# A graph network of two layers: in the attention layer VectorE's two 1280-wide passes change places, and TensorE turns the scores before it sums over edges

## The reference

```
h = relu(layernorm(x));  x = x + attention(h)      # 4 heads of 32
h = relu(layernorm(x));  x = x + messages(h)

attention:
  q, k, v = h@Wq+bq, h@Wk+bk, h@Wv+bv
  alpha[e,head] = sum_c q[dst]*k[src] / sqrt(32)
  alpha = softmax of alpha over the edges with one dst
  out[n] = sum over edges into n of v[src]*alpha  +  h@Wskip + bskip
```

## Time and profile before

| what | value |
|---|---|
| median of 3 timed runs | 1677.4 us (1675.71 to 1679.96) |
| the profiled execution, from first to last instruction | 2119.4 us |
| table stage, in the profile | 0 to about 344 us |
| attention layer | about 344 to 1204 us |
| start of the message layer | about 1204 to 1303 us |
| message layer | about 1303 to 2107 us |
| busy over the span: PE, DVE, ACT, POOL | 75%, 66%, 49%, 47% |

### The profile page before, as it was taken

The page is one execution under the profiler, slowest core; times in us unless marked ns, Lnnn a source line. Parts: engine busy times, 40 slices in busy tenths (PEclk is TensorE's granted clock), DMA queues, the critical chain, the costliest instruction groups (busy, mean ns, idle before and its releaser), DMA issues.

```text
span 2119.4 us, 34578 instructions
## 1 busy us (share of the span) xinstructions
PE 1596.5 (75%) x10545; PEld 1337.9 (63%) x10546; DVE 1390.2 (66%) x3977; ACT 1036.2 (49%) x2500; POOL 990.1 (47%) x1021
## 2 busy tenths in 40 slices
PE   5879964877788777778877515877788887788887
PEld 4667753767777777777776414666566665666665
DVE  8998951777778777777778703555555555555565
ACT  6668963444444444444444023544444444444453
POOL 0100005655566566656664074555555555555530
PEclk9989996999999999999999757999888888777789
DMA  8778974445454555545454233545444445444442
GB/s 239 242 237 275 316 231 123 124 137 150 127 148 137 144 148 140 148 132 147 135 146 127 62 96 72 129 118 122 120 116 116 119 119 123 123 119 121 117 109 62
DMA packets 162399, 302.86 MB, mean 143 GB/s; under 512 B 104084, under 2 KB 107674, under 8 KB 157245
## 3 DMA queue, kind: packets, MB, share of 16 engines
q1 hardware_dynamic: 121349, 201.19, 32.6%
q0 software_dynamic: 40896, 99.90, 18.7%
HBM read 196.84 MB, written 104.12 MB: 142 GB/s over the span
## 4 chain that ended last, share of the span: by engine, by line
PE 47%; DVE 19%; issue 17%; another core or an unknown queue 10%; DMA 2%; ACT 2%; SPq 1%; DVEq 0%; ACTq 0%
PE ps_b L1769 6%; PE ps_b L1877 5%; PE ps_b L1888 5%; PE ps_b L1889 5%; PE ps_b L1890 5%; PE ps_b L1865 4%; PE ps_b L1899 4%; PE ps_b L1670 3%; DVE sb_member L1055 2%; PE ps_b L1802 2%; PE ps_b L1876 2%; PE ps_b L1757 2%; DVE sb_st L833 1%; DVE sb_kv L854 1%
## 5 line engine op out<-in xcount | busy, mean ns | idle before, releaser
L749 POOL DMA_INDIRECT sb_kv<-kv_rows,sb_src_all x500 | 504.1, 1008 | 542.2 <-DMA kv_rows<-sb_kv 207.1
L777 POOL DMA_INDIRECT sb_kv<-x_rows,sb_src_all x500 | 473.3, 947 | 420.1 <-ACT sb_vw L1586 228.8
L1583 ACT ACTIVATE sb_hn<-sb_xn 100x128 f32<-100x128 f32 x500 | 243.7, 487 | 498.4 <-PE ps_b L1877 241.8
L1274 DVE COPY sb_hT<-ps_b 128x400 f32<-128x400 f32 x250 | 142.2, 569 | 202.3 <-remote 155.0
L1586 ACT ACTIVATE sb_vw<-sb_kv 128x128 f32<-128x128 f32 x500 | 241.1, 482 | 0.0
L1511 ACT ACTIVATE sb_hn<-sb_xn,sb_nstat 100x128 f32<-100x128 f32 x500 | 231.7, 495 | 13.7 <-DMA sb_xn<-in_x 13.7
L1899 PE MATMUL ps_b<-sb_ident,sb_q 128*100 128x128 f32 x500 | 99.8, 324 | 156.6 <-issue 111.7
L1670 PE MATMUL ps_b<-sb_w,sb_memberT 128*125 128x256 f32 x800 | 203.1, 392 | 17.3 <-DVE sb_kv L854 13.9
L1802 PE MATMUL ps_b<-sb_vw,sb_member 128*100 128x128 f32 x1000 | 139.4, 290 | 68.2 <-DVE sb_vw L1115 68.2
L1533 ACT COPY sb_memberT<-ps_b 100x512 f32<-100x512 f32 x150 | 76.4, 510 | 217.8 <-PE ps_b L1757 113.4
L1877 PE MATMUL ps_b<-sb_member,sb_vw 128*128 128x100 f32 x1000 | 176.0, 280 | 0.0
(11 more groups left out here) (172 smaller groups left out, 3420.1 us busy)
## 6 DMA issues: line engine op xcount, KB each, us to landing
kv_rows<-sb_kv SPq DMA_DIRECT2D x27, 1120.0 KB
sb_xn<-x_rows SPq DMA_DIRECT2D x50, 507.8 KB
sb_xn<-in_x SPq DMA_DIRECT2D x50, 500.0 KB
out_rows<-sb_xo SPq DMA_DIRECT2D x49, 500.0 KB
x_rows<-sb_xo SPq DMA_DIRECT2D x24, 1015.6 KB
sb_kv<-in_edge_attr SPq DMA_DIRECT2D x500, 32.0 KB
sb_kv<-in_x SPq DMA_DIRECT2D x28, 560.0 KB
kv_rows<-sb_xn SPq DMA_DIRECT2D x13, 1120.0 KB
```

Source lines behind the costliest of these rows:

```text
L749: pool.indirect_dma_start(out=kvs[:, k % 4, t, :], out_offset=None, in_=kv_rows, in_offset=bass.IndirectOffsetOnAxis(ap=src_all[:, n:n + 1 ...
L777: pool.indirect_dma_start(out=xs1[:, k % 4, t, :], out_offset=None, in_=x1, in_offset=bass.IndirectOffsetOnAxis(ap=src_all[:, n:n + 1], ax ...
L1583: nc.scalar.activation(hn1[:, t, :], xn1[:, k % 4, t, 0:D], ACT.Relu, scale=xn1[:, k % 4, t, D:D + 1], bias=xn1[:, k % 4, t, D + 1:XW]).th ...
```

## The change

On DVE `head_sums(k)` now comes ahead of `weigh(k-1)`, with the tiny step `stats(12)` between them as before. On PE `turn_alpha(k)` moves from behind the last `aggregate(k-1, 2)` to ahead of `aggregate(k-1, 0)`. No instruction, size, wait or buffer is changed, and `last_steps` stays.

```
@@ DVE, step0 @@
                 if this:
                     scores(k, 2)
                 stats(11)
+                if this:
+                    head_sums(k)
+                stats(12)
                 if prev:
                     weigh(k - 1)
-                stats(12)
-                if this:
-                    head_sums(k)
                 stats(13)
                 if nxt:
                     members(k + 1, 1)
@@ PE, step0 @@
                     skip(k - 1, 0)
                     skip(k - 1, 1)
+                if this:
+                    turn_alpha(k)
+                if prev:
                     aggregate(k - 1, 0)
                     aggregate(k - 1, 1)
                     skip(k - 1, 2)
                     aggregate(k - 1, 2)
-                if this:
-                    turn_alpha(k)
                 if nxt:
                     turn_member(k + 1, 1)
```

## The result

The changed kernel takes 1709.37 us (1707.76 to 1710.52), the kernel before 1677.67 us (1675.71 to 1679.96): 31.7 us more, a ratio of 1.0174 with a 95% interval of 1.0152 to 1.0195. I had forecast 1712, 35 more.

A forecast was written before the change was run, and what follows sets the result against it. DVE was taken to set the pace in the attention layer; 25 steps x 0.67 plus 23 x 0.81 gave 35 us on 1677.4, so 1712. Likeliest case 1697 to 1727, 8 in 10 1668 to 1727.

The forecast's parts named there:

- the sum over the stages: Whole kernel: undisturbed stages add to 1719 us, against 1909 with the profile's attention layer; timed runs 1677.4.
- the long waits before `weigh`: DVE, attention layer: 88.9 us over 41 waits in the profile, claimed to be hardly in the timed runs.
- the profile after would look no worse: Changed kernel's profile against the first profile's 2119.4 us: 27 us less, about 2092, while timed runs are slower.
- The waits of `finish`: DVE, attention layer: two new gaps, 0.64 us before `finish(k-1, 0)` and 0.27 before `finish(k-1, 1)`.
- The step: Attention layer: each step 0.67 us longer without norm work, 0.81 with it.
- none elsewhere in it: DVE in the late model step of 13.09 us: idle 0.24 us before `weigh` and nowhere else.
- The count: Attention layer: 23 steps with norm work x 0.81 plus 25 without x 0.67, 35 us in all.
- The first: Rival: the wait before `weigh` is in the timed runs too and covering it wins, 27 us, 1650; chance 0.18.
- The second: Rival: another engine, PE or POOL, sets the pace and hides the DVE gaps, 1677 to 1695; chance 0.16.
- The third: Rival: PE's results are seen late by `finish`, 0.3 us and more a step, 1727 or above; chance 0.08.

The follow-up runs named there:

- Experiment 1: The kernel before, unchanged, run again for a second profile: 1680.87 us, with a profile span of 1679.0.
- experiment 3: The kernel before with only the PE half of the change, `turn_alpha(k)` ahead of `aggregate(k-1, 0)`: ratio 1.0137 to the kernel before.
- Experiment 7: The kernel before with `turn_member(k+1, 1)` and `(k+1, 2)` moved on PE between `aggregate(k-1, 1)` and `skip(k-1, 2)`: 1664.53 us, ratio 0.9901.
- experiment 4: The changed kernel with `members(k+1, 1)` also moved ahead of `weigh(k-1)` on DVE: ratio 1.0339 to the kernel before.

## Why the prediction was right

**Which execution to model.** The step on which all else hung: the profile given didn't match the timed runs, and the sum over the stages said that the long waits before `weigh` weren't in them. Experiment 1 shows it. The sum itself was partly lucky: it came out 42 us high, with larger errors inside it that pulled against each other. By the second profile the message layer takes 12.64 us a step and not 11.76 (43 us too little in the sum), and the way from the layer's last `finish` to that layer's first (L1300) 38 us, where the odd profile had 95. Its attention layer, 670, was close: 664 from the first `wr` to the end of the last `finish`. Priced by that profile's own rows the change would have come out 27 us faster, the wrong sign. The forecast that the profile after would look no worse, near 2092, failed with it: it came at 1705.9. I had taken the long waits for a feature of profiling; they belong to one execution, and what caused them there isn't known.

**The waits of `finish`.** Forecast 0.64 and 0.27, reckoned from start to start. Reckoned so, the runs show 0.73 (728.53 to 729.95, less the 0.69 of `members`) and 0.27 (729.95 to 730.82, less 0.60); the idle column, which leaves out the overlap of rows, has 0.64 and 0.18. The 0.09 missing from the first is the transpose: I let it start 0.06 behind the end of `weigh`, as the sum does, and it starts 0.14 behind, so the sum begins 0.25 behind that end and not 0.17. (In experiment 3, where it waits for `head_sums`, it does start 0.06 behind; why it is later here isn't known.) `finish(k-1, 0)` came 2.81 after `weigh` began, 2.74 forecast.

**The step.** Forecast 0.67 longer without norm work and 0.81 with it; measured 0.75 and 0.62. The mean is right to 0.05, but partly by luck, since terms that I had missed cancel.

- On one side `head_sums` can't follow `scores(k, 2)` by 0.33: it needs its result and follows by 0.45. And there is the 0.09 of the transpose.
- On the other, "none elsewhere in it" was wrong: the late step that I took as the model had a pair of `scores` of 1.49 us too, where undisturbed it takes 1.27, and the pair began 0.12 later than it could. Those were waits for `gather_q`, and the changed kernel, with DVE later, no longer has them. I read the idle column, which is empty for a pair merged into one row, and not the pair's length. Experiment 7 shows that they and the wait before `weigh` were worth some 14 of its 17 us.
- A tiny instruction (the last section) got 0.2 us slower in the steps without norm work and 0.17 faster in the others. Without it the first kind would have come out cheaper than forecast (0.55) and the second near it (0.79); over the layer it cancels to 1 us.

**The count.** 48 steps: 25 x 0.75 + 23 x 0.62 = 33 us, and from its first `wr` to its last the layer grew from 654.3 to 688.2, by 33.9. The two profiles' spans differ by 26.9 only, since the changed kernel's execution was 2.9 us ahead at the first `wr` (342.8, against 345.7) and took 4.1 less after the last. The timed runs differ by 31.7.

**The rivals.** The first (the wait is real, 1650) fell with experiment 1. The second (PE or POOL hides it): the granted clock is 0.99 in the layer and POOL waits for `weigh` 44.1 us in all, so neither was near. The third (a dearer wait) fell too: the first group's sum is seen 1.08 us after its start (728.87 to 729.95), as the forecast had it (1171.20 to 1172.28).

## What to carry to other kernels

Putting work ahead of a wait gains at most that wait, and it delays everything that hangs on the instruction put off; ask first what that instruction had to spare at its reader (here 0.62 us) and what covered the reader's own latency, for one piece of cover can't stand in both places. When a profile is far longer than the timed runs, add up undisturbed steps and compare with the clock before pricing anything by its waits. And the rows of a full engine deserve a look at distances between starts, since a merged row hides an idle time inside.

## What the runs showed of the hardware

DVE's tiny `tot + 1e-16` (L1104, a TENSOR_SCALAR from SBUF to SBUF, 40x128) takes 0.22 us in most steps and 0.32 to 0.48 in others. What decides is where it falls in one of POOL's gathers. From the second profile of before:

```profile
720.76 0.95 POOL L749 DMA_INDIRECT sb_kv<-kv_rows,sb_src_all  x1 [0.30 <-issue]
721.36 0.40 DVE L1104 TENSOR_SCALAR sb_tot_e<-sb_tot 40x128 f32<-40x128 f32 x1
```

and from experiment 4:

```profile
728.54 0.95 POOL L749 DMA_INDIRECT sb_kv<-kv_rows,sb_src_all  x1 [0.30 <-issue]
729.04 0.22 DVE L1104 TENSOR_SCALAR sb_tot_e<-sb_tot 40x128 f32<-40x128 f32 x1
```

The first begins 0.35 us before its gather ends and is done 0.05 us behind that end; the second begins 0.45 us before the end and isn't slowed. It is so in all eleven profiles of this case, 50 instructions in each: the 153 slow ones began 0.27 to 0.43 us before the end of a gather and ended 0.04 to 0.05 us behind it; the 397 others, outside a gather or elsewhere in one, took 0.22. So which kind of step pays changes with the phase of POOL against DVE. In the second profile of before 23 were slow, 22 of them in steps with norm work; in the changed kernel 23, all in steps without; in experiment 4 none, though 43 of the 50 begin inside a gather. The Trainium skill (SBUF — State Buffer, "SBUF: two separate sides") has DVE and GpSimd share a pair of ports by an exclusive lock, which whoever starts first holds for its whole instruction. A wait that lasts until the gather's end agrees with a lock; that the lock is held for the whole gather does not fit, since an instruction that begins earlier in one isn't held up. No run here took the gathers away.
